# First loads of x in smaller groups, Pool's order of steps, and the place of one weight load in a fused attention and expert kernel

## The chip, the cores and the metric

One core of a Trainium2 chip runs the whole program. Its engines work side by side and meet at semaphores: TensorE (PE, with weight loads as PEld), VectorE (DVE), ScalarE (ACT), GpSimd (Pool) and SyncE (SP), which here only issues DMAs. The metric is the device time of one execution in microseconds (us).

## The reference

The input x is [2, 2048, 256]. Two blocks follow each other, each wrapped as x + layernorm(block(layernorm(x))).

```python
def attn(x):                       # softmax-free attention
    h = layernorm(x) * norm_w + norm_b
    q, k, v = split(h @ qkv_w.T + qkv_b)
    o = (q @ k.T / sqrt(C)) @ v
    return x + o @ proj_w.T + proj_b

def ffn(x):                        # soft mixture of 64 experts, 32 slots each
    logits = einsum('bmd,dnp->bmnp', x, phi)
    dispatch = softmax(logits, axis=0)            # over the batch
    combine = softmax(logits over all n * p)
    slots = einsum('bmd,bmnp->bnpd', x, dispatch)
    y = einsum('bnpd,nde->bnpe', slots, W) + b
    return einsum('bnpd,bmnp->bmd', y, combine)

x = x + layernorm(attn(layernorm(x)))
x = x + layernorm(ffn(layernorm(x)))
```

## The kernel before

Batch b holds 16 tiles of 128 tokens (`NJ` = 16), x lies in `xres[:, b, j, :]`, and t = 16 b + j numbers the 32 tiles. As the attention has no softmax, the kernel builds for each batch the 256 x 256 matrix S of products of normalised rows, and from it and two products of weights (G and U) one matrix A, by which the rows are then multiplied. The stages are:

1. Up to about 46 us: load, statistics, S and the transposed rows, products of weights, A. The change lies here.
2. Up to about 108 us: rows times A (`h_pair`), `add_x`, the norms behind it, the first products with phi.
3. Up to the end: blocks over the experts, then the weighted sum over them and the stores.

Every engine has its own hand-written order of instructions. Nothing is reordered when the program runs; an engine stands at each `wait_ge` until the semaphore is high enough.

**SP** issues loads in this order: five x groups (`X_GROUPS`: tiles 0-1, 2-3, 4-7, 8-11, 12-15 of batch 0; line 352), then `w_raw`, `wbc`, `bbc`, `qbc`, `wpT` (lines 356 to 360, all on `par_loaded`), the four groups of batch 1 (line 352 again), phi (363) and the first expert weights (365). ScalarE's queue issues `proj_b` and `bT` (664, 665).

**VectorE** works through `stats(g)` for each group: one `bn_stats` (L993) and one `bn_aggr` (L996) a tile. Its order is stats 0 to 4, `proj_bias`, `weight_scale` (waits for `par_loaded`; L1008), stats 5, `bias_columns` (six L1002), `primed_weights` (L1036, which gives the first `wprime_ready`), `centre_projection` (L1012 to L1016 on `wpT`, the second `wprime_ready`), stats 6 to 8. After that it takes the largest magnitude of phi, waits for TensorE to spread it (`phi_turn`, `phi_broadcast`), and splits phi into two halves of 16 bits (L1087, L1091). Only then comes the first `add_x` (L1103).

**Pool** turns each group's mean and variance into a scale and an offset in `x_terms(g)`: variance plus epsilon (L504), the power -1/2 (L492), the negative mean (L507), their product (L509, which raises `n1_ready`). Behind all nine groups it runs `residual_terms(b)` for both batches: L516, L517, a power over 16 columns (L492) and the product L521. Their readers are `add_x` and `y_squares` of stage 2. Then come a 16-bit identity and constants for a fold.

**ScalarE** makes the normalised rows: `xhat(t)` (L687) waits for `n1_ready` of its group and, from t = 4, for a free one of four buffers. Its order is xhat(2p), xhat(2p + 1), then the copy of the transposed pair p - 2 (L671). For p = 8 the copy of S of batch 0 stands between these two.

**TensorE** runs 14 warm-up products (`WARM`), then `s_tile(t)` for t = 0 to 31: two products into S (L1453) and two transposes (L1460). Before the transposes of an even tile it waits for the copy of the pair two back. Between the tiles stand the bias rows (after t = 7), `weight_products` and `T_step(0)` (after 17), `R_step(0)` (19), `A_step(0)` (21), `phi_turn` (22) and `phi_broadcast` (24, L1472). `h_pair` (L1511) follows after tile 31.

Of the kernel before, what the change touches and what calls it, by code (L numbers as in the profile page):

```python
# [22 lines left out]
ALU = mybir.AluOpType  # L23
# [4 lines left out]
P = 128  # L28
# [63 lines left out]
def build(nc, x, norm_w, norm_b, qkv_w, qkv_b, proj_wT, proj_b, phi, ffn_w, ffn_bT, out):  # L92
    B, T, C = x.shape
# [3 lines left out]
    NJ = T // P  # L97
# [4 lines left out]
    TB = 512 // P  # L102
    EP = P // Q
    GJ = 4
    XG = B * NJ // GJ
    NG = NJ // GJ
    assert (B, K, TB) == (2, 2, 4)

    x_v = x.rearrange("b (p j) c -> p b j c", j=NJ)
# [7 lines left out]
    with ExitStack() as ctx:  # L117
        def sb(name, shape, dt=F32):
            return ctx.enter_context(nc.sbuf_tensor(name, shape, dt))

        def sem(name):
            return ctx.enter_context(nc.semaphore(name))


        xres = sb("xres", [P, B, NJ, C])
# [44 lines left out]
        wpT = a.take(K * C).rearrange("p (k c) -> p k c", k=K)  # L170
# [53 lines left out]
        mvx = sm.take(64).rearrange("p (b j s) -> p b j s", b=B, j=NJ)  # L224
# [29 lines left out]
        bk = [psM[:, i * 512:(i + 1) * 512] for i in range(4)]  # L254


        par_loaded, rows_loaded = sem("par_loaded"), sem("rows_loaded")
        x_loaded = [sem(f"x_loaded{g}") for g in range(XG + 1)]
        phi_loaded = sem("phi_loaded")
        W_loaded = [sem(f"W_loaded{i}") for i in range(2)]  # L260
        pool_const = sem("pool_const")
# [52 lines left out]
        out_stored = [sem(f"out_stored{i}") for i in range(2)]  # L314

        y_lots = [(1, 0), (1, 1), (0, 0), (0, 1), (1, 2), (0, 2), (1, 3), (0, 3)]
        N_PAR = 5


        X_GROUPS = [(0, 0, 2), (0, 2, 2)] + [(b, j, GJ) for b in range(B) for j in range(0, NJ, GJ) if b + j]  # L320
        GROUP_OF = {(b, j + i): g for g, (b, j, n) in enumerate(X_GROUPS) for i in range(n)}


# [25 lines left out]
        def _(sp):  # L349
            def load_x(g):  # L350
                b, j, n = X_GROUPS[g]
                sp.dma_start(xres[:, b, j:j + n, :], x_v[:, b, j:j + n, :]).then_inc(x_loaded[g], 16)

            for g in range(NG + 1):
                load_x(g)
            sp.dma_start(w_raw, qkv_w.rearrange("(s p) c -> p s c", p=P)).then_inc(par_loaded, 16)
            sp.dma_start(wbc, norm_w.rearrange("(o c) -> o c", o=1).broadcast_to([P, C])).then_inc(par_loaded, 16)
            sp.dma_start(bbc, norm_b.rearrange("(o c) -> o c", o=1).broadcast_to([P, C])).then_inc(par_loaded, 16)
            sp.dma_start(qbc, qkv_b).then_inc(par_loaded, 16)
            sp.dma_start(wpT, proj_wT.rearrange("(k p) e -> p k e", p=P)).then_inc(par_loaded, 16)  # L360
            for g in range(NG + 1, XG + 1):
                load_x(g)
            sp.dma_start(phf, phi_v).then_inc(phi_loaded, 16)
            for w in range(2):
# [93 lines left out]
        def _(pool):  # L458
            own = Count(pool, pool_own)
# [29 lines left out]
            def rsqrt(o, v):  # L489

                n = v.shape[1]
                return nc.gpsimd.tensor_tensor(o, v, epst[:, 0:1].broadcast_to([P, n]), ALU.pow)  # L492
# [3 lines left out]
            def x_terms(g):  # L496

                b, j, n = X_GROUPS[g]
                tn = slice(j, j + n)
                e2, nm = ve[:, g % 2 * 8:g % 2 * 8 + n], ve[:, g % 2 * 8 + GJ:g % 2 * 8 + GJ + n]  # L500
                pool.wait_ge(stats_x, g + 1)
                if g >= 2:
                    pool.wait_ge(n1_ready, g - 1)
                own.add(nc.gpsimd.tensor_scalar(e2, mvx[:, b, tn, 1], 1.0 + EPS, EPS * EPS, ALU.mult, ALU.add))  # L504
                own.wait()
                own.add(rsqrt(r1[:, b, tn], e2))
                own.add(nc.gpsimd.tensor_scalar(nm, mvx[:, b, tn, 0], -1.0, 0.0, ALU.mult, ALU.add))  # L507
                own.wait()
                nc.gpsimd.tensor_tensor(n1[:, b, tn], nm, r1[:, b, tn], ALU.mult).then_inc(n1_ready, 1)  # L509

            def residual_terms(b):

                e1, nm = ve[:, 16:32], ve[:, 32:48]
                if b:
                    pool.wait_ge(r0_ready, b)
                own.add(nc.gpsimd.tensor_scalar(e1, mvx[:, b, :, 1], EPS, 1.0, ALU.add, ALU.mult))  # L516
                own.add(nc.gpsimd.tensor_scalar(nm, mvx[:, b, :, 0], -1.0, 0.0, ALU.mult, ALU.add))  # L517
                own.wait()
                own.add(rsqrt(r0[:, b], e1))
                own.wait()  # L520
                nc.gpsimd.tensor_tensor(n0[:, b], nm, r0[:, b], ALU.mult).then_inc(r0_ready, 1)  # L521

            for g in range(XG + 1):
                x_terms(g)
            residual_terms(0)
            residual_terms(1)
            pool.wait_ge(r0_ready, 2)
            nc.gpsimd.tensor_scalar(ident16, ident, 1.0, 0.0, ALU.mult, ALU.add).then_inc(ident16_ready, 1)
# [132 lines left out]

        @block.scalar
        def _(act):
            act.dma_start(pb_rows[Q - 1:Q], proj_b.rearrange("(o c) -> o c", o=1)).then_inc(rows_loaded, 16)
            act.dma_start(bT[:, :, :], ffn_bT.rearrange("(k p) n -> p k n", p=P)).then_inc(rows_loaded, 16)

# [305 lines left out]
        def _(dve):  # L972
            own = Count(dve, dve_own)
# [12 lines left out]
            def stats(g):  # L986

                b, j, n = X_GROUPS[g]
                dve.wait_ge(x_loaded[g], 16)
                if g >= 2:  # L990
                    dve.wait_ge(stats_x, g - 1)
                for i in range(n):
                    own.add(V.bn_stats(stat[:, g % 2, i, :], xres[:, b, j + i, :]))  # L993
                own.wait()
                for i in range(n):
                    ins = V.bn_aggr(mvx[:, b, j + i, :], stat[:, g % 2, i, :])  # L996
                ins.then_inc(stats_x, 1)
# [7 lines left out]
            def weight_scale():  # L1005

                dve.wait_ge(par_loaded, 16 * N_PAR)
                own.add(V.tensor_tensor(w_aug, w_raw, wbc.unsqueeze(1).broadcast_to([P, KS, C]), ALU.mult))  # L1008

            def centre_projection():  # L1010

                own.add(V.tensor_reduce(wm, wpT, AX_X, ALU.add))  # L1012
                own.wait()
                own.add(V.tensor_scalar(wm, wm, 1.0 / C, None, ALU.mult))
                own.wait()
                V.tensor_tensor(wpT, wpT, wm.unsqueeze(2).broadcast_to([P, K, C]), ALU.subtract).then_inc(wprime_ready, 1)  # L1016

            def proj_bias():

                dve.wait_ge(rows_loaded, 32)  # L1020
                dve.wait_ge(pool_const, 2)
                own.add(V.tensor_reduce(pbm[P - Q:P, 0:1], pb_rows, AX_X, ALU.add))
                own.wait()
                own.add(V.tensor_scalar(pbm[P - Q:P, 1:2], pbm[P - Q:P, 0:1], 1.0 / C, None, ALU.mult))
                own.wait()
                own.add(V.tensor_scalar(pb_rows, pb_rows, pbm[P - Q:P, 1:2], None, ALU.subtract))
# [11 lines left out]
                own.wait()  # L1038
                V.tensor_tensor(w_aug[:, :, C - 1], bcol, qbc, ALU.add).then_inc(wprime_ready, 1)

            stats(0)
            stats(1)
            stats(2)
            stats(3)
            stats(4)
            proj_bias()
            weight_scale()
            stats(5)
            own.add(V.tensor_reduce(bmx, bT.rearrange("p k n -> p (k n)"), AX_X, ALU.max, apply_absolute_value=True))
            bias_columns()  # L1050
            primed_weights()
            centre_projection()
            stats(6)
            stats(7)
            stats(8)

            def pow2_scale(i, top, least, done):

# [768 lines left out]
```

## Time and profile before

| | us |
|---|---|
| median of three runs | 641.18 |
| lowest and highest of them | 640.73, 641.26 |
| the profiled execution, whole | 641.88 |
| its span in the profile | 640.1 |
| TensorE busy in the span | 628.2 |
| VectorE, ScalarE, Pool busy | 447.9, 359.0, 230.2 |

Times in the views count from the start of the span. A line such as L1036 is that line of the kernel. On TensorE, a busy stretch need not be one at full pace, since the ends of its instructions are modelled. The releaser in brackets is inferred from semaphores: it is what came last before an engine went on.

### The profile page before, as it was taken

The numbers are of one execution on the slowest core, as the hardware profiler recorded it, in microseconds if no ns is written. First come the engines' busy times: TensorE is split into PE (matmuls) and PEld (weight loads), VectorE is DVE, ScalarE is ACT, GpSimd is POOL, SyncE is SP. The second block draws the span as 40 slices with busy tenths as digits, with TensorE's granted clock in tenths as the row PEclk, the third lists the DMA queues.
The fourth block names the chain that finished last, engine by engine and source line by source line (L and its number), as shares of the span: only waits on it lengthen the run. The fifth ranks groups of instructions, "written<-read, shape, count | busy, mean of one in ns | idle before, by whom it ended". The sixth has DMA issues, their size and how long they took to land.

```text
span 640.1 us, 15341 instructions
## 1 busy us (share of the span) xinstructions
PE 628.2 (98%) x5351; PEld 395.4 (62%) x5351; DVE 447.9 (70%) x857; ACT 359.0 (56%) x694; POOL 230.2 (36%) x410
## 2 busy tenths in 40 slices
PE   8999999999999999999999999999999999999996
PEld 8898644545444444444444457777777777777776
DVE  5978888835244453446344399999888888888886
ACT  5666776843233232224444356777777777777764
POOL 5375896820000000000000001555555555555554
PEclk9999999999999999999999999999999999999999
DMA  8920032325766666666555531222222222222201
GB/s 266 402 77 1 1 67 50 67 60 156 201 176 176 177 193 185 173 178 203 135 136 186 159 104 67 91 90 90 90 90 90 90 90 90 90 90 90 90 16 34
DMA packets 78485, 77.07 MB, mean 120 GB/s; under 512 B 6386, under 2 KB 74995, under 8 KB 76147
## 3 DMA queue, kind: packets, MB, share of 16 engines
q1 hardware_dynamic: 76112, 74.48, 38.4%
q10 hardware_dynamic: 2338, 2.16, 1.0%
q8 instruction: 19, 0.31, 0.2%
q14 instruction: 16, 0.12, 0.1%
HBM read 51.71 MB, written 23.07 MB: 117 GB/s over the span
## 4 chain that ended last, share of the span: by engine, by line
PE 79%; DVE 8%; POOL 5%; issue 3%; DMA 2%; ACT 2%; SPq 1%; DVEq 0%; POOLq 0%; ACTq 0%
PE psL L1568 24%; PE psM L1555 11%; PE psL L1687 11%; PE psM L1705 7%; PE psM L1709 7%; PE psM L1706 7%; PE psM L1585 3%; POOL small L492 2%; DMA r_xn<-in_proj_wT 2%; PE psL L1773 1%; PE psL L1453 1%; PE psM L1511 1%; DVE phs L1091 1%; DVE small L1286 1%; DVE r_xn L1305 1%
## 5 line engine op out<-in xcount | busy, mean ns | idle before, releaser
L1568 PE MATMUL psL<-r,r_xn 128*128 128x512 f16 x768 | 176.3, 379 | 0.8 <-DVE r L1112 0.8
L1568 PEld LDWEIGHTS psL<-r,r_xn 128*128 128x128 f16 x768 | 73.4, 98 | 91.0 <-issue 7.0
L762 ACT ACTIVATE r<-psM,small 128x512 f32<-128x512 f32 x64 | 43.7, 682 | 96.3 <-PE psM L1555 95.5
L1555 PE MATMUL psM<-phs,xx 128*128 128x512 f16 (+1 forms) x384 | 93.2, 379 | 0.9 <-DVE xx L1146 0.9
L580 POOL MEMSET r_xn<- 128x8 f16 x2 | 0.3, 137 | 234.2 <-PE psL L1568 234.2
L1110 DVE TENSOR_SCALAR r<-r 128x512 f16<-128x512 f32 x64 | 28.5, 445 | 71.8 <-ACT r L762 71.8
L1687 PE MATMUL psL<-phs,r 128*32 128x512 f16 x1344 | 75.1, 379 | 0.0
L1555 PEld LDWEIGHTS psM<-phs,xx 128*128 128x128 f16 x384 | 37.3, 98 | 45.9 <-DVE xx L1146 1.4
L875 ACT ACTIVATE r<-psL,small 128x512 f32<-128x512 f32 x60 | 41.9, 776 | 37.7 <-DVE small L1313 37.4
L492 POOL TENSOR_TENSOR small<-small,epst 128x2 f32<-128x2 f32 (+3 forms) x75 | 59.8, 797 | 6.2
L1687 PEld LDWEIGHTS psL<-phs,r 128*32 128x32 f16 x1344 | 34.6, 97 | 36.5 <-issue 3.0
L875 ACT ACTIVATE r_xn<-r_xn,small 128x512 f32<-128x512 f32 x64 | 47.1, 824 | 1.3 <-DVE small L1313 1.3
L1112 DVE SCALAR_TENSOR_TENSOR r<-r 128x512 f16<-128x512 f32 x64 | 46.1, 721 | 2.2
L597 POOL TENSOR_SCALAR small<-small 128x1 f32<-128x1 f32 x30 | 20.5, 682 | 69.6 <-ACT r L910 69.3
L1286 DVE TENSOR_REDUCE small<-psL 128x1 f32<-128x512 f32 x60 | 38.2, 684 | 6.0 <-PE psL L1687 6.0
L671 ACT ACTIVATE r<-psM 128x512 f32<-128x512 f32 (+1 forms) x67 | 39.1, 585 | 4.8 <-PE psM L1611 3.2
L1272 DVE STREAM_TRANSPOSE xx<-r_xn 128x1024 f32<-128x1024 f32 x32 | 39.1, 1228 | 2.3 <-ACT r_xn L875 1.5
L585 POOL TENSOR_TENSOR r<-xx,r 128x1024 f16<-128x1024 f32 x15 | 32.0, 2136 | 19.8 <-DVE r_xn L1264 19.8
L1305 DVE CUSTOM_DVE_ANT_0 r_xn<-psL,xx 128x512 f32<-128x512 f32 x60 | 37.9, 687 | 1.6 <-issue 0.6
L1272 DVE STREAM_TRANSPOSE r<-r 128x1024 f32<-128x1024 f32 x32 | 38.1, 1225 | 0.5 <-ACT r L875 0.4
L1264 DVE TENSOR_TENSOR r_xn<-r,r_xn 128x1024 f16<-128x1024 f32 x32 | 37.2, 1202 | 0.1
L1232 DVE TENSOR_TENSOR r_y<-psM,r 128x512 f32 (+1 forms) x12 | 8.3, 692 | 41.0 <-PE psM L1585 41.0
(200 smaller groups left out, 1260.8 us busy)
## 6 DMA issues: line engine op xcount, KB each, us to landing
r<-in_ffn_w SPq DMA_DIRECT2D x23, 1024.0 KB, 5.8
logit_difference<-r SPq DMA_DIRECT2D x256, 64.0 KB, 1.9
xx<-logit_difference SPq DMA_DIRECT2D x16, 1024.0 KB, 4.8
out<-r SPq DMA_DIRECT2D x32, 128.0 KB, 1.7
xres<-in_x SPq DMA_DIRECT2D x7, 512.0 KB, 11.4
r<-in_phi SPq DMA_DIRECT2D x1, 2048.0 KB, 19.3
expert_bias<-r ACTq DMA_DIRECT2D x1, 2048.0 KB, 21.6
r<-expert_bias SPq DMA_DIRECT2D x16, 128.0 KB, 5.5
```

The lines of the kernel that those rows point to most:

```text
L492: return nc.gpsimd.tensor_tensor(o, v, epst[:, 0:1].broadcast_to([P, n]), ALU.pow)
L875: nc.scalar.activation(E[b][:, c], src[:, c], ACT.Exp, bias=ebias[:, w, g:g + 1], scale=kap[:, 0:1]).then_inc(E_ready[b], 1)
L1112: V.scalar_tensor_tensor(thl[:, j % 2, 1], tF[:, j % 2], S_SCALE, thl[:, j % 2, 0], ALU.mult, ALU.subtract).then_inc(s_split, 1)
L1272: V.transpose(ET[b].rearrange("p (t g r) -> p g t r", g=GJ, r=Q)[:, g2], E[b].rearrange("p (g t c) -> p g t c", g=GJ, c=Q)[:, g2]).then_in ...
L1286: own.add(V.tensor_reduce(lmax[:, 0, g:g + 1], logits_at(j)[:, 512 * g:512 * g + 512], AX_X, ALU.max))
L1305: V.tensor_tensor_reduce(E0[:, c], logits_at(j)[:, c], dB[:, c], 1.0, -3.0e38, ALU.add, ALU.max, lmax[:, 1, g:g + 1]).then_inc(l_added, 1)
L1555: ins = mm(bk[j % 2][:, :].rearrange("p (q m) -> p q m", q=EP), xxT[:, 1, j, hx, k, :], phw[:, hp, k, :, bass.ds(nb, 1), :].rearrange("p q ...
L1568: ins = mm(psL[:, i * 512:(i + 1) * 512], x3n[:, b, j, hx, k * P:(k + 1) * P], thl[:, j % 2, hs, :], start=(j == 0 and hx + hs == 0), stop ...
L1687: ins = mm(logits_at(j)[q * Q:(q + 1) * Q, g * 512:(g + 1) * 512], xj[:, hx, k, g * Q:(g + 1) * Q], phs[:, hp, k, q * 512:(q + 1) * 512], ...
L1705: mm(acc, eT[b][:, 0, t, :], yh(b, t), start=first, stop=False)
L1706: mm(acc[:, 0:C], eT[b][:, 0, t, :], yl(b, t), start=False, stop=False)
L1709: return mm(acc, eT[b][:, 1, t, :], yh(b, t), start=False, stop=last)
```

## The change

- The groups of x in batch 0 become tiles 0, 1, 2-3, 4-5, 6-7, 8-11, 12-15; those of batch 1 stay. There are eleven groups (`XG`), seven of them in batch 0 (`NG`).
- Tile 1's load is issued from ScalarE's queue, ahead of its two others.
- `wpT` has its own semaphore, `wpT_loaded`. `weight_scale` waits for four loads instead of five, and `centre_projection` waits for `wpT`. On SP the load of `wpT` stands behind batch 1's first group.
- In `x_terms` on Pool the negative mean stands ahead of the power.
- `residual_terms(0)` moves on Pool from behind all groups to behind batch 0's groups.

```diff
+    X_GROUPS = [(0, 0, 1), (0, 1, 1), (0, 2, 2), (0, 4, 2), (0, 6, 2)] + [
+        (b, j, GJ) for b in range(B) for j in range(0, NJ, GJ) if b or j >= 2 * GJ]
+    XG = len(X_GROUPS)
+    NG = XG - NJ // GJ
...
-        N_PAR = 5
-        X_GROUPS = [(0, 0, 2), (0, 2, 2)] + [(b, j, GJ) for b in range(B) for j in range(0, NJ, GJ) if b + j]
+        N_PAR = 4
...
-            for g in range(NG + 1):
-                load_x(g)
+            for g in range(NG):
+                if g != 1:
+                    load_x(g)
...
-            sp.dma_start(wpT, proj_wT.rearrange("(k p) e -> p k e", p=P)).then_inc(par_loaded, 16)
-            for g in range(NG + 1, XG + 1):
+            load_x(NG)
+            sp.dma_start(wpT, proj_wT.rearrange("(k p) e -> p k e", p=P)).then_inc(wpT_loaded, 16)
+            for g in range(NG + 1, XG):
                 load_x(g)
...
                 own.add(nc.gpsimd.tensor_scalar(e2, mvx[:, b, tn, 1], 1.0 + EPS, EPS * EPS, ALU.mult, ALU.add))
+                own.add(nc.gpsimd.tensor_scalar(nm, mvx[:, b, tn, 0], -1.0, 0.0, ALU.mult, ALU.add))
                 own.wait()
                 own.add(rsqrt(r1[:, b, tn], e2))
-                own.add(nc.gpsimd.tensor_scalar(nm, mvx[:, b, tn, 0], -1.0, 0.0, ALU.mult, ALU.add))
                 own.wait()
...
-            for g in range(XG + 1):
+            for g in range(NG):
                 x_terms(g)
             residual_terms(0)
+            for g in range(NG, XG):
+                x_terms(g)
             residual_terms(1)
...
+            act.dma_start(xres[:, 0, 1:2, :], x_v[:, 0, 1:2, :]).then_inc(x_loaded[1], 16)
...
             def centre_projection():
 
+                dve.wait_ge(wpT_loaded, 16)
                 own.add(V.tensor_reduce(wm, wpT, AX_X, ALU.add))
...
-            stats(0)
-            stats(1)
-            stats(2)
-            stats(3)
-            stats(4)
+            for g in range(NG):
+                stats(g)
             proj_bias()
             weight_scale()
-            stats(5)
+            stats(NG)
...
-            stats(6)
-            stats(7)
-            stats(8)
+            for g in range(NG + 1, XG):
+                stats(g)
```

## Rows read from the trace of the kernel before

**Rows 1.** Chain that ended last, in order of time: start us, us, what
```profile
6.06 10.88 DMA r_xn<-in_proj_wT
...
39.39 0.32 PE psM L1472 x2
...
49.55 0.40 DVE r_y L1103
```

**Rows 2.** Timeline, TensorE: start, duration us, line, out<-in, count [idle before <-releaser]
```profile
1.90 5.93 PE L1516 MATMUL psM<-r 128*128 128x128 f32 x28 [1.90 <-POOL r L468]
...
7.67 0.82 PE L1453 MATMUL psL<-r 128*128 128x256 f32 x4
...
8.54 0.82 PE L1453 MATMUL psL<-r 128*128 128x256 f32 x4
...
12.24 0.44 PE L1460 MATMUL psM<-r 128*128 128x128 f32 x2
...
24.84 0.44 PE L1460 MATMUL psM<-r 128*128 128x128 f32 x2 [0.49 <-ACT xx L671]
...
56.68 3.72 PE L1511 MATMUL psL<-r,xx 128*128 128x256 f32 x16 [0.21 <-DVE r L1031]
```

**Rows 3.** Timeline, ScalarE: tiles 16 and 17
```profile
22.78 1.09 ACT L687 ACTIVATE r<-xres,small 128x255 f32<-128x255 f32 x2 [1.22 <-POOL small L509]
```

**Rows 4.** Timeline, VectorE: weight scaling, statistics, bias columns, primed weights
```profile
16.96 1.76 DVE L1008 TENSOR_TENSOR r_xn<-r_xn 128x1536 f32<-128x1536 f32 x1 [3.75 <-DMA r_xn<-in_proj_wT]
...
18.64 1.40 DVE L993 BATCH_NORM_STATS2 stat<-xres 128x6 f32<-128x256 f32 x4
...
20.54 0.41 DVE L1002 CUSTOM_DVE_ANT_0 r<-r_xn 128x256 f32<-128x256 f32 x1
...
22.72 1.75 DVE L1036 TENSOR_TENSOR r_xn<-r_xn 128x1530 f32<-128x1530 f32 x1
```

**Rows 5.** Timeline, Pool: first groups, tile 16's group, residual terms
```profile
5.06 0.19 POOL L504 TENSOR_SCALAR small<-small 128x2 f32<-128x2 f32 x1 [2.85 <-DVE small L996]
...
6.32 0.19 POOL L509 TENSOR_TENSOR small<-small 128x2 f32<-128x2 f32 x1
...
6.60 0.19 POOL L504 TENSOR_SCALAR small<-small 128x2 f32<-128x2 f32 x1
...
8.81 0.20 POOL L504 TENSOR_SCALAR small<-small 128x4 f32<-128x4 f32 x1 [0.78 <-DVE small L996]
...
10.66 0.20 POOL L504 TENSOR_SCALAR small<-small 128x4 f32<-128x4 f32 x1
...
20.54 0.47 POOL L504 TENSOR_SCALAR small<-small 128x4 f32<-128x4 f32 x1 [6.29 <-DVE small L996]
...
22.47 0.27 POOL L509 TENSOR_TENSOR small<-small 128x4 f32<-128x4 f32 x1
...
33.51 0.21 POOL L516 TENSOR_SCALAR small<-small 128x16 f32<-128x16 f32 x1
...
37.38 0.44 POOL L516 TENSOR_SCALAR small<-small 128x16 f32<-128x16 f32 x1
```

**Rows 6.** DMA issues (KB each, median us to landing), then SP's queue in time
```profile
xres<-in_x SPq DMA_DIRECT2D x7, 512.0 KB, 11.4
...
small<-in_qkv_b SPq DMA_DIRECT2D x1, 3.0 KB, 9.1
...
5.52 0.50 SPq L359 DMA_DIRECT2D small<-in_qkv_b  x1
...
6.81 3.51 SPq L352 DMA_DIRECT2D xres<-in_x  x4
```

**Rows 7.** Timeline, Pool and VectorE near 504 us, far behind the change
```profile
504.03 1.28 POOL L601 TENSOR_TENSOR small<-small 128x1 f32<-128x1 f32 x1
...
504.05 1.22 DVE L1264 TENSOR_TENSOR r<-xx,r 128x1024 f16<-128x1024 f32 x1
```

**Rows 8.** Timeline, Pool: terms of x3, mean ahead of power
```profile
54.28 0.19 POOL L552 TENSOR_SCALAR small<-small 128x2 f32<-128x2 f32 x1 [0.60 <-DVE small L1132]
...
55.88 0.19 POOL L539 TENSOR_SCALAR small<-small 128x2 f32<-128x2 f32 x1
```

**Rows 9.** Timeline, VectorE: phi's split, one instruction a row
```profile
40.69 0.48 DVE L1087 TENSOR_SCALAR phs<-r,small 128x512 f16<-128x512 f32 x1
...
41.08 0.48 DVE L1087 TENSOR_SCALAR phs<-r,small 128x512 f16<-128x512 f32 x1
...
44.09 0.75 DVE L1091 SCALAR_TENSOR_TENSOR phs<-r,small,phs 128x512 f16<-128x512 f32 x1
```

More of the change, by code:

```diff
@@ L104, in build @@
     GJ = 4
-    XG = B * NJ // GJ
-    NG = NJ // GJ
+    X_GROUPS = [(0, 0, 1), (0, 1, 1), (0, 2, 2), (0, 4, 2), (0, 6, 2)] + [
+        (b, j, GJ) for b in range(B) for j in range(0, NJ, GJ) if b or j >= 2 * GJ]
+    XG = len(X_GROUPS)
+    NG = XG - NJ // GJ
     assert (B, K, TB) == (2, 2, 4)
@@ L254, in build @@
         bk = [psM[:, i * 512:(i + 1) * 512] for i in range(4)]
-        par_loaded, rows_loaded = sem("par_loaded"), sem("rows_loaded")
-        x_loaded = [sem(f"x_loaded{g}") for g in range(XG + 1)]
+        par_loaded, rows_loaded, wpT_loaded = sem("par_loaded"), sem("rows_loaded"), sem("wpT_loaded")
+        x_loaded = [sem(f"x_loaded{g}") for g in range(XG)]
         phi_loaded = sem("phi_loaded")
```

## The prediction

> **What bounds the kernel now.** I read the chain that ended last in order of time, then the timelines of the engines over its first 50 us. TensorE's work and what it waits for carry the span, and the part that the change touches ends at about 50 us. The chain begins with the landing of `wpT` at 6.06 + 10.88 = 16.94 us, because `par_loaded` counts all five parameter loads. From there it runs through VectorE, Pool and ScalarE to TensorE's tile 16, then along TensorE's own order to the broadcast of phi's top at 39.39, and through VectorE's split of phi to the first `add_x` at 49.55 [rows 1]. On TensorE's timeline the reader sees this [rows 2]. The 14 warm-up products fill TensorE from 1.90 to about 7.6, and tile 0 starts at 7.67. After that one tile takes 8.54 - 7.67 = 0.87 us. There are two visible hold-ups: the transposes of tile 4 start at 12.24, and those of tile 16 at 24.84 after 0.49 us of idle. At tile pace tile 4 would start at 7.67 + 4 x 0.87 = 11.15 and its transposes at 11.8, so about 0.44 us was lost there. At tile 16, `xhat` started at 22.78, waiting for Pool's L509 [rows 3, 5]; that wait ends last.
>
> **The change, part by part.** All sums go against the profiled execution (span 640.1 us, whole run 641.88 us) as a difference, which I then put on the median of 641.18 us.
>
> **Smaller first loads, one of them on ScalarE's queue.** Half a group saves one statistics instruction of 1.40 / 4 = 0.35 us [rows 4] and about 0.1 us of aggregation. Pool's first term then starts at 5.06 - 0.45 = 4.6 us, or 4.2 us if 128 KB also lands 0.4 us sooner. `xhat` of tile 0 is ready some 0.6 us sooner, but tile 0 is queued behind the warm-up to 7.6 us, so nothing is gained at the start. If that cover were gone it would be worth 0.5 to 0.9 us. Against it stands Pool's pace. A group of two costs 6.60 - 5.06 = 1.54 us [rows 5], and there are now five groups ahead of tile 8 where there were three. Tiles 2 and 3 come third on Pool: 4.2 + 3 x 1.6 = 9.0 us against a need at 7.67 + 2 x 0.87 = 9.4 less `xhat`'s 0.59, so TensorE loses about 0.2 us there and wins back part of the 0.44 at tile 4. By tile 8 I count a gain of 0 to 0.5, likeliest 0.1 us, and it dies at tile 16 in any case unless tile 16's terms come sooner too. ScalarE's extra issue of about 0.5 us falls in its idle first 6 us. The two row loads behind it (`proj_b`, `bT`) move by as much; their reader on VectorE stands just ahead of L1008, where VectorE sat idle for 3.75 us [rows 4].
>
> **Pool's negative mean ahead of its power.** The same three steps and the product, in another order. Pool runs one instruction at a time, so nothing is hidden. The later helper already has the new order: 55.88 - 54.28 = 1.60 us a group [rows 8], against 1.54 in the old one [rows 5]. That is +0.06 us a group; the value for `x_terms` is taken as 0 to +0.06.
>
> **Weights' last load behind x of batch 1.** `weight_scale` now waits for four loads. The last of them, `qbc`, was issued at 5.52 and took 9.1 us: 14.6 us [rows 6]. SP issues one x load more ahead of it but the bytes in front are the same, so 14.6 to 15.1. VectorE's L1008 moves from 16.96 to about 14.65 and ends at 14.65 + 1.76 = 16.4 [rows 4]. Next comes `stats` of the first group of batch 1. Of the seven 512 KB loads the median landing, 11.4 us, is the fourth issued, which went out at 6.81: 18.2 us [rows 6], 1.27 us behind `wpT` for 512 KB. With `wpT`'s 256 KB behind it rather than ahead it lands about 0.63 us sooner: 17.6 (to 18.2). So stats start at 17.6 rather than 18.64 and are ready for Pool at 17.6 + 1.9 = 19.5 rather than 20.54 [rows 4, 5]. `wpT` then lands at 18.2, and its reader is due after 23 us: free. VectorE's L1036 keeps its distance of 22.72 - 18.64 = 4.08 us from these stats and so runs from 21.7 to 23.4 [rows 4].
>
> **`residual_terms(0)` ahead of batch 1's terms.** It costs Pool 37.38 - 33.51 = 3.87 us [rows 5]; it leaves a place where nobody waited for it and enters a place ahead of tile 16's terms. A group of four takes 10.66 - 8.81 = 1.85 us today [rows 5], 1.91 in the new order, so Pool ends batch 0's terms near 4.2 + 2 x 1.56 + 3 x 1.6 + 2 x 1.9 = 15.9 us (1.56 for a group of one is an estimate between the two orders). If nothing disturbed it the residual terms would end at 19.8, just as tile 16's statistics are ready. But now L1008 runs beside Pool. Far behind, near 504 us, the trace shows what that does: a Pool product of one column, of 0.19 us on quiet ground (L509 at 6.32) [rows 5], took 1.28 us beside a VectorE product with two SBUF inputs of 1.22 us, and both ended together [rows 7]. L1008 is of that kind, and used to run within the 6.29 us in which Pool stood idle [rows 5]. Pool's L509 of the last group, due at about 15.7, therefore ends at about 16.55. The residual terms run from 16.65 to 20.5, and tile 16's terms start at 20.5, no sooner than today.
>
> From there today's distance to L509 is 22.47 - 20.54 = 1.93 us [rows 5], which gives 22.45. Today L509 slips in 0.25 us ahead of L1036. After the change L1036 starts at 21.7 and L509 falls into it: it ends at about 23.55. `xhat` of tile 16 starts at 23.6 rather than 22.78, **0.82 us later**, and TensorE's transposes with it. TensorE is dense from there to phi's broadcast, so the delay stays.
>
> The Trainium skill, "SBUF — State Buffer", section "Who interferes with whom", says that a VectorE instruction with two SBUF inputs and a GpSimd instruction that reads SBUF exclude each other for the whole instruction. By that rule the trace agrees, with 1.28 us; without such a lock the change would come out at the first rival below.
>
> **What comes back.** Pool's last terms, identity and fold constants end up to 3.87 + 1 us sooner, with the residual terms gone from their front, and so leave phi's split alone. L1087's pace is 41.08 - 40.69 = 0.39 us where Pool is quiet, but the eight took 44.09 - 40.69 = 3.40 us [rows 9]: 0.28 us is returned. TensorE's h pairs see +0.82 less the 0.21 us for which TensorE waits for VectorE at 56.68 today [rows 2], so 0.54 to 0.61 whichever of the two is late there. **The sum** for what follows is +0.82 - 0.25 = about +0.6 us. Later stages hang on these engines and not on loads, so I carry it unchanged: 641.18 + 0.6 = 641.8 us.
>
> **Rivals.** First, Pool is not held up: L1008 lands on Pool's long power, which takes its inputs at once. Then tile 16's terms start at 19.5 to 19.8, `xhat` at 21.75 to 22.0, and by today's distance of 24.84 - 22.78 = 2.06 us [rows 2, 3] TensorE's transposes at 23.8 to 24.1, 0.75 to 1.0 us sooner. What is late next is S's copy behind tile 15, so 0.5 to 0.95 us; with 0.25 from phi's split, 640.0 to 640.4. For it speaks that VectorE's six L1002 (22.72 - 20.54 = 2.18 us [rows 4]) ran undelayed beside a Pool power; against it that the short steps come between. Second, and on the other side: the power of tile 16's terms itself comes behind L1036. It is issued 0.85 us after the terms start, at 21.35, with L1036 at 21.7. If Pool is over 0.35 us later than I count, or x lands that much sooner, the power waits to 23.4 and L509 ends at 24.85: +2.1 - 0.25 = 1.85 us, so 643.0. Third, batch 1's x lands at 18.4 or later, L1036 starts behind L509, and only the 0.25 of phi's split is left: 640.9. Last, the loads don't land sooner at all, `qbc`'s small packets being the limit: L1008 near 15.5, everything 0.8 us later on Pool, L509 behind L1036 at 24.0 or so: +1.0, 642.2.
>
> **How the numbers follow.** Chances: forecast 0.42 (641.4 to 642.4), first rival 0.20, slower rival 0.20, third 0.10, last 0.08. The range 640.0 to 643.1 takes in the ends of all but some 0.2. A difference under 0.2% (1.28 us) is about what a measurement of this kernel can't tell from no change. Beyond it on the fast side lies about half of the first rival, with a little for load times that I can't see: 0.13. Beyond it on the slow side lie the slower rival and the upper tails of the forecast and of the last: 0.27. The rest, 0.60, is no difference.
>
> **What would show it.** In the profile of the changed kernel: tile 0 at 7.67 as today; L1008 near 14.7; a Pool L509 of over 0.8 us beside it; the residual terms ending at about 20.5; another long L509 beside L1036, ending near 23.5; `xhat` of tile 16 at 23.6; phi's eight L1087 in 3.2 us; the first `add_x` some 0.5 us later than 49.47. The forecast is wrong if Pool's steps beside L1008 and L1036 keep their 0.2 us, or if tile 16's terms start before 20 us.

## The result: slower by 0.4%

| | median us | lowest to highest | runs | ratio to before, 95% interval |
|---|---|---|---|---|
| before | 641.18 | 640.64 to 641.63 | 7 | |
| changed | 643.97 | 642.38 to 645.08 | 7 | 1.0044 [1.0032, 1.0055] |

The changed kernel takes 2.8 us more, where 0.6 was forecast and 643.1 was the upper end. Its runs also spread over 2.7 us where those of before spread over 1.0. The profiled execution took 643.97 us, with a span of 642.0. One execution of a later kernel, at a mean clock of 0.852, took 728.45 us and is in no median here.

Pool's timeline (start us, duration us, line, instruction) holds the cause. L512 is the last step of a group's terms, L519 to L524 are the residual terms of batch 0, and L507 is the first step of tile 16's terms:

```profile
14.85 1.01 POOL L495 TENSOR_TENSOR small<-small,epst 128x4 f32<-128x4 f32 x1
15.94 1.79 POOL L512 TENSOR_TENSOR small<-small 128x4 f32<-128x4 f32 x1
17.81 0.20 POOL L519 TENSOR_SCALAR small<-small 128x16 f32<-128x16 f32 x1
...
21.36 0.35 POOL L524 TENSOR_TENSOR small<-small 128x16 f32<-128x16 f32 x1
21.80 1.68 POOL L507 TENSOR_SCALAR small<-small 128x4 f32<-128x4 f32 x1
23.56 0.20 POOL L508 TENSOR_SCALAR small<-small 128x4 f32<-128x4 f32 x1
23.84 1.01 POOL L495 TENSOR_TENSOR small<-small,epst 128x4 f32<-128x4 f32 x1
24.92 0.29 POOL L512 TENSOR_TENSOR small<-small 128x4 f32<-128x4 f32 x1
```

VectorE's timeline of the same stretch has the two long products of the weights, `weight_scale` and `primed_weights`:

```profile
15.91 1.76 DVE L1014 TENSOR_TENSOR r_xn<-r_xn 128x1536 f32<-128x1536 f32 x1 [2.14 <-DMA small<-in_qkv_b]
17.58 1.40 DVE L999 BATCH_NORM_STATS2 stat<-xres 128x6 f32<-128x256 f32 x4
...
21.67 1.75 DVE L1043 TENSOR_TENSOR r_xn<-r_xn 128x1530 f32<-128x1530 f32 x1
```

Two Pool steps that take 0.2 us elsewhere took 1.79 and 1.68 us: each lasted until the VectorE product beside it had ended (at 17.67 and 23.42). Together they are 3.1 us longer than quiet ones. Beside the statistics, which read one tile from SBUF and not two, L519 took its usual 0.20 us. The terms of tile 16 were ready at 25.2 instead of 22.74 [rows 5]. ScalarE and TensorE follow:

```profile
25.24 1.09 ACT L693 ACTIVATE r<-xres,small 128x255 f32<-128x255 f32 x2 [3.59 <-POOL small L512]
```

```profile
25.90 1.65 PE L1456 MATMUL psL<-r 128*128 128x256 f32 x4 [2.31 <-ACT r L693]
27.34 0.65 PE L1463 MATMUL psM<-r 128*128 128x128 f32 x2
27.79 1.45 PE L1456 MATMUL psL<-r 128*128 128x256 f32 x4
29.07 0.39 PE L1463 MATMUL psM<-r 128*128 128x128 f32 x2
29.29 1.89 PE L1440 MATMUL psM<-r_xn 128*128 128x256 f32 x8
```

`xhat` of tile 16 is 25.24 - 22.78 = 2.46 us later than before [rows 3]. TensorE then runs two tiles at half pace: the four records of a tile's first products last 1.65 and 1.45 us where they took 0.82 [rows 2]. The stages show why (stretch, length, then busy time and count of TensorE, its weight loads, VectorE, ScalarE and Pool, then the granted clock, the DMA share and GB/s):

```profile
23.50:25.90 2.40, 0.09 (x2) 0.01 (x1) 2.33 (x7) 0.66 (x2) 1.49 (x3) 0.95 1.05 390
25.90:26.90 1.00, 1.00 (x2) 0.84 (x3) 0.97 (x7) 1.00 (x4) 0.00 (x0) 0.50 1.06 381
26.90:27.90 1.00, 1.00 (x6) 0.94 (x5) 1.00 (x4) 1.00 (x3) 0.77 (x3) 0.50 1.09 392
27.90:28.90 1.00, 1.00 (x5) 0.82 (x5) 0.96 (x7) 0.81 (x2) 0.84 (x3) 0.50 1.09 389
```

After 2.31 us without work the granted clock was 0.50, the lower of the two levels (1.2 of 2.4 GHz), for some 3 us. From the transposes of tile 16 to the products of weights TensorE needed 29.29 - 27.34 = 1.95 us. Before, these products began at 25.98 on the same view, 1.14 us behind the transposes [rows 2]:

```profile
25.98 1.89 PE L1437 MATMUL psM<-r_xn 128*128 128x256 f32 x8
```

So the clock costs 0.81 us, and TensorE is 2.5 + 0.8 = 3.3 us late. That lateness is still there at the start of stage 2:

```profile
52.59 1.65 DVE L1106 SCALAR_TENSOR_TENSOR r_y<-xres,small,psM 128x256 f32<-128x256 f32 x4
```

The first `add_x` starts 52.59 - 49.47 = 3.12 us later. The missing 0.2 us is phi's split, undisturbed by Pool.

At the end the spans of the two profiled executions differ by only 1.9 us, though the medians differ by 2.8. The profiled execution of before (641.88 us, 0.7 over its median) carries a wait of TensorE of 0.92 us in stage 2, and a second one of 0.27 us at 95.44, that the changed kernel's lacks: 3.1 - 1.2 = 1.9. The first row is before, the second the run with primed_weights alone in pieces, below, which has it too:

```profile
91.11 1.47 PE L1555 MATMUL psM<-phs,xx 128*128 128x512 f16 x6 [0.92 <-DVE xx L1146]
```

```profile
90.95 1.47 PE L1559 MATMUL psM<-phs,xx 128*128 128x512 f16 x6 [0.92 <-DVE xx L1150]
```

The other profiled executions don't have the wait at 91 us. The run with the residual terms back, for one, has TensorE at the same point as before at 78 us (77.92 against 77.97), and its span is 638.9 us against 640.1. So one profiled execution of a kernel can stand 1 us from another, and the medians are the measure here. What decides whether this wait comes was not tested.

### The profile page after: what moved, and what is told of

Same layout as the page of the kernel before. It is cut to its first block, busy times and chain, and to the rows that moved or that the text cites. A ratio compares the mean times of both kernels' runs of the same rounds, so it can differ in the third digit from the quotient of the medians.

```text
span 642.0 us, 15355 instructions
## 1 busy us (share of the span) xinstructions
PE 628.8 (98%) x5351; PEld 395.9 (62%) x5351; DVE 447.7 (70%) x857; ACT 359.0 (56%) x694; POOL 231.7 (36%) x418
## 4 chain that ended last, share of the span: by engine, by line
PE 81%; POOL 7%; DVE 6%; issue 3%; ACT 1%; DMA 0%; POOLq 0%; DVEq 0%; ACTq 0%
PE psL L1571 24%; PE psM L1558 11%; PE psL L1690 11%; PE psM L1708 7%; PE psM L1712 7%; PE psM L1709 7%; PE psM L1588 3%; POOL small L495 3%; PE psL L1456 2%; PE psM L1514 1%; PE psL L1776 1%; PE psL L1514 1%; DVE small L1289 1%; POOL r_xn L568 1%; DVE r_xn L1308 1%
## 5 line engine op out<-in xcount | busy, mean ns | idle before, releaser
L602 POOL TENSOR_SCALAR small<-small 128x1 f32<-128x1 f32 x30 | 20.6, 686 | 69.6 <-ACT r L916 69.3
```

## Experiments

**Theory A:** a Pool instruction that reads SBUF waits out a VectorE instruction with two SBUF inputs. The change brings Pool into two such products one after the other: the sooner `weight_scale` meets the end of batch 0's terms, the residual terms hand the delay on to tile 16's terms, and these fall into `primed_weights`. The rivals were the order of the loads, the small groups with Pool's pace, the residual terms as such, and (for the last 0.8 us) something other than the clock. Medians of before beside these runs were 641.01, 640.96 and 641.04.

### The residual terms back in their place

```diff
-            for g in range(NG):
+            for g in range(XG):
                 x_terms(g)
             residual_terms(0)
-            for g in range(NG, XG):
-                x_terms(g)
             residual_terms(1)
```

> The changed kernel with residual_terms(0) put back on Pool behind all groups; the rest of the change stays. In the changed kernel the first step of tile 16's terms (L507) started at 21.80 and took 1.68 us beside VectorE's L1043, and xhat of tile 16 started at 25.24 against 22.78 before. Theory A (Pool is held up by VectorE products with two inputs from SBUF, and the residual terms push tile 16's terms into the second of them): tile 16's terms start at 19.5 and are through before 21.7, xhat of tile 16 starts at 21.6 to 21.8, TensorE keeps its clock, and the time is 0.5 to 1.2 us below before: 640.0 to 640.7. Rival B (the smaller first groups or the new order of loads cost the time): L507 of tile 16 still ends after 23 us and the time stays near 643 to 644.

640.83 us, ratio 0.9998 [0.9989, 1.0007]: all of the loss is gone, but the time is above the expected 640.0 to 640.7. Pool still meets the first product and is then free in time for tile 16's statistics:

```profile
16.02 1.28 POOL L512 TENSOR_TENSOR small<-small 128x4 f32<-128x4 f32 x1
19.06 0.47 POOL L507 TENSOR_SCALAR small<-small 128x4 f32<-128x4 f32 x1 [1.76 <-DVE small L1000]
```

ScalarE started `xhat` of tile 16 at 21.63, as Theory A said. But the gain of 0.5 to 1.2 us that I expected from it didn't come. TensorE's transposes of tile 16 started at 24.80, against 24.84 before, because ScalarE's next copies wait for tile 15:

```profile
23.70 0.55 ACT L675 ACTIVATE r_xn<-psL 128x128 f32<-128x128 f32 x2 [0.99 <-PE psM L1461]
24.14 0.60 ACT L675 ACTIVATE xx<-psM 128x512 f32<-128x512 f32 x1
```

The two copies of S can't start before tile 15 is done, and the copy of transposed pair 6, on which TensorE's transposes wait, stands behind them. In the trace of before, tile 15 was done at 23.10 + 0.38 = 23.48 and the copies of S started at 23.77, so at most 0.3 us was to be had:

```profile
23.10 0.38 PE L1460 MATMUL psM<-r 128*128 128x128 f32 x2
```

```profile
23.77 0.52 ACT L671 ACTIVATE r_xn<-psL 128x128 f32<-128x128 f32 x2
```

Sooner terms for tile 16 are worth next to nothing. Later ones cost in full: in the profiled executions with `xhat` of tile 16 at 22.78 or later and these copies in their old order, the transposes start 2.06 us behind it (2.10 in the changed kernel, where the clock fell).

### The residual terms alone, on the kernel before

```diff
-            for g in range(XG + 1):
+            for g in range(NG + 1):
                 x_terms(g)
             residual_terms(0)
+            for g in range(NG + 1, XG + 1):
+                x_terms(g)
             residual_terms(1)
```

> The kernel before with residual_terms(0) alone moved on Pool to behind batch 0's groups. Theory A: Pool was idle from 14.25 to 20.54, so the residual terms run from 14.3 to about 18.2; only their last product meets L1008 (16.96 to 18.7) and ends by 18.8, ahead of tile 16's statistics at 20.5. xhat of tile 16 stays at 22.8; with Pool quiet during phi's split 0.1 to 0.3 us is gained: 640.9 to 641.1. Rival C (the move of the residual terms costs by itself, wherever VectorE's products stand): xhat of tile 16 later than 23.5 and 642.5 or more.

640.82 us, ratio 0.9996 [0.9987, 1.0005], against 641.01. The gain of 0.19 us is of the size expected and inside the noise (the time is 0.1 us under the expected range). Pool's one meeting with L1010 (16.67 to 18.4) cost 0.58 - 0.22 = 0.4 us where nobody waited:

```profile
17.93 0.58 POOL L521 TENSOR_TENSOR small<-small 128x16 f32<-128x16 f32 x1
20.25 0.47 POOL L504 TENSOR_SCALAR small<-small 128x4 f32<-128x4 f32 x1 [1.74 <-DVE small L998]
```

So the move is harmless by itself; it did harm only together with the sooner `weight_scale`.

### wpT's place alone, on the kernel before

```diff
-            sp.dma_start(wpT, ...).then_inc(par_loaded, 16)
-            for g in range(NG + 1, XG + 1):
+            load_x(NG + 1)
+            sp.dma_start(wpT, ...).then_inc(wpT_loaded, 16)
+            for g in range(NG + 2, XG + 1):
                 load_x(g)
```

Not shown: `weight_scale` waits for four loads, `centre_projection` for `wpT_loaded`, as in the changed kernel.

> The kernel before with wpT's load alone moved behind batch 1's first group and taken out of par_loaded (one semaphore of its own). Theory A: the products weight_scale start at 15 to 16 us, batch 1's first statistics at 17.6, Pool's terms of tile 16 at 19.5, xhat of tile 16 at 21.5 to 21.8. What is late next is the copy of S behind tile 15 (ends 23.3), so TensorE gains 0.4 to 0.6 us and the time is 640.4 to 640.8. Rival B: the new order of loads costs the time: xhat of tile 16 not sooner than 22.8 and the time 641.2 or more.

640.91 us, ratio 1.0001 [0.9991, 1.0010]. `weight_scale` started at 15.09 and `xhat` of tile 16 at 21.86, about as Theory A said (21.5 to 21.8), but TensorE again waited 0.48 us for the same copy (transposes at 25.02). The expected 0.4 to 0.6 us didn't come (the time is above 640.4 to 640.8), for the reason found in the first run. The order of loads doesn't cost anything either.

### VectorE's two long products in six pieces each

```diff
-                own.add(V.tensor_tensor(w_aug, w_raw, wbc..., ALU.mult))
+                for s in range(KS):
+                    own.add(V.tensor_tensor(w_aug[:, s, :], w_raw[:, s, :], wbc, ALU.mult))
...
-                own.add(V.tensor_tensor(w_aug[:, :, 0:C - 1], ..., ALU.subtract))
+                for s in range(KS):
+                    own.add(V.tensor_tensor(w_aug[:, s, 0:C - 1], w_aug[:, s, 0:C - 1],
+                                            w_aug[:, s, C - 1:C]..., ALU.subtract))
```

> The changed kernel with VectorE's two long products (weight_scale L1014 and primed_weights L1043, 1.75 us each) written as six products of 256 columns each. The work is the same. Theory A (whoever holds the shared ports holds them for one instruction): Pool's steps beside them take at most 0.5 us instead of 1.79 and 1.68, the terms of tile 16 end near 22.5, xhat of tile 16 starts at 22.3 to 22.9, TensorE keeps its clock, and the time is within 0.5 us of before: 640.7 to 641.5. Rival D (Pool waits for VectorE's whole stretch, or for something else that comes with it): the steps stay at 1.5 us or more, xhat of tile 16 at 25 us, 643 to 644.

640.73 us, ratio 0.9999 [0.9990, 1.0009]: every part of the change is in place, and its whole loss is gone. VectorE is 2.12 us over the first product instead of 1.76 (15.43 to 17.55), and 2.09 over the second (from 21.61). Pool's steps:

```profile
15.98 0.28 POOL L512 TENSOR_TENSOR small<-small 128x4 f32<-128x4 f32 x1
16.34 0.26 POOL L519 TENSOR_SCALAR small<-small 128x16 f32<-128x16 f32 x1
...
20.34 0.25 POOL L507 TENSOR_SCALAR small<-small 128x4 f32<-128x4 f32 x1
20.67 0.27 POOL L508 TENSOR_SCALAR small<-small 128x4 f32<-128x4 f32 x1
21.02 1.07 POOL L495 TENSOR_TENSOR small<-small,epst 128x4 f32<-128x4 f32 x1
22.17 0.26 POOL L512 TENSOR_TENSOR small<-small 128x4 f32<-128x4 f32 x1
```

The first two and the last two of these rows stand beside pieces, for the power of tile 16's terms (21.02) in part. The same work in shorter instructions leaves them 0.05 to 0.08 us of delay a step; in the later runs with pieces a short step beside them took up to 0.46 us. The two rows between (0.25 and 0.27 us) stand beside the bias columns, VectorE instructions of 0.4 us that also read two inputs from SBUF. It is the length of the single VectorE instruction that Pool waits out. The Trainium skill says so in "SBUF — State Buffer", section "Who interferes with whom" (the pair is held for the whole instruction), and the run agrees for VectorE as the holder. For Pool's power as the holder the runs differ from it, and they decide (last section).

### Only one of the two products in pieces

> The changed kernel with only primed_weights' product (the later one) in six pieces. Theory A: the first collision stays (a Pool step of 1.3 to 1.8 us beside weight_scale), so tile 16's terms start near 21.3 to 21.8 as in the changed kernel, but no step beside primed_weights takes over 0.5 us: xhat of tile 16 at 23.3 to 23.9, 1.4 us sooner than 25.24, TensorE idle under 1 us and its clock kept: 641.3 to 642.2. Rival K: one collision is as dear as both: 643 or more.

> The changed kernel with only weight_scale's product (the sooner one) in six pieces. Theory A: Pool is through batch 0's terms and the residual terms by about 20.0 to 20.4, tile 16's terms start at 20.4 and their last step (L512) is due at 22.2, beside primed_weights (21.6 to 23.4), so it takes about 1.2 us: xhat of tile 16 at 23.5 (the course that the prediction forecast). 641.3 to 642.2. Rival L: the first product is the whole cause, and without that delay nothing meets the second: xhat of tile 16 at 22.5, 640.7 to 641.0.

Only `primed_weights` in pieces: 641.59 us, ratio 1.0015 [1.0006, 1.0025]. Only `weight_scale` in pieces: 641.51 us, ratio 1.0011 [1.0002, 1.0019]. Both are in the ranges expected. By the medians each of these kernels loses about 0.5 us, where the one with both products whole loses 2.8. With only `weight_scale` in pieces the second meeting stands alone:

```profile
20.17 0.34 POOL L524 TENSOR_TENSOR small<-small 128x16 f32<-128x16 f32 x1
20.60 1.68 POOL L507 TENSOR_SCALAR small<-small 128x4 f32<-128x4 f32 x1
```

Tile 16's terms started at 20.6, near the 20.4 expected, but it was their first step that fell behind the product, not their last: the loads had landed sooner, `weight_scale` ran from 14.37, and `primed_weights` started at 20.47 instead of 21.6. So the second meeting comes in full without the first. `xhat` came at 24.05 instead of 23.5, 3.58 us behind the start of `primed_weights`, as in the changed kernel (25.24 - 21.67 = 3.57): once the first step is held, only the place of this product counts.

In the other run the first meeting was shorter than expected (L512 0.84 us, with `weight_scale` from 14.75), and `xhat` came at 22.79, sooner than the 23.3 expected. The transposes of tile 16 started at 24.85, so in this profile the first meeting cost TensorE nothing; its time of 641.88 us has the wait at 91 us. One execution of each of the two kernels (643.88 and 643.91 us) had a mean clock of 0.997, as the slower ones of the changed kernel, so a fall of the clock seems not to need both meetings. How the 2.8 us of the medians split between the two meetings, the landing of the loads and the clock isn't shown.

### TensorE kept busy while it waits

```diff
             for t in range(B * NJ):
+                if t == NJ:
+                    for i in range(9):
+                        mm(bk[0][:, 0:P], ident[:, :], ident[:, :], start=True, stop=True)
                 s_tile(t)
```

> The changed kernel with nine more warm-up products (128 columns each, 0.21 us at full pace, about 1.9 us in all) on TensorE between tiles 15 and 16, where it stood idle for 2.31 us. They compute nothing that is used. Theory A2: the two tiles behind the idle time ran at the lower clock (granted 0.50 from 25.9 to 28.9, a tile's first products 1.65 us instead of 0.82), and that cost comes on top of the 2.46 us by which xhat of tile 16 was late. With TensorE busy the clock stays at 1.0, tile 16's transposes wait for ScalarE to about 27.3 and the products of weights start at 28.4 instead of 29.3: 0.8 to 0.9 us less than the changed kernel, about 643.1 by its median of 643.97. Rival E: the clock is not what costs there, or falls all the same: no difference from the changed kernel, 643.7 to 644.2.

642.68 us, ratio 1.0029 [1.0020, 1.0039], 1.3 us less than the changed kernel (1.1 with each against its own before), with useless work added. The clock stayed at 1.00 from 23.5 to 30 (one stretch of it, columns as above), and the way from the transposes to the products of weights is 27.94 - 26.79 = 1.15 us again:

```profile
25.90:26.90 1.00, 0.51 (x4) 0.30 (x3) 0.96 (x7) 1.00 (x4) 0.37 (x2) 1.00 1.08 390
```

```profile
26.79 0.44 PE L1463 MATMUL psM<-r 128*128 128x128 f32 x2 [0.49 <-ACT xx L677]
27.06 0.82 PE L1456 MATMUL psL<-r 128*128 128x256 f32 x4
27.72 0.38 PE L1463 MATMUL psM<-r 128*128 128x128 f32 x2
27.94 1.89 PE L1440 MATMUL psM<-r_xn 128*128 128x256 f32 x8
```

So 0.8 us is the clock. Between the two profiled executions (643.97 and 642.64 us) the other 0.5 is a sooner landing in this one (L1014 at 15.39, `xhat` at 24.73). Its runs span 642.17 to 643.36; the two fastest of the seven of the changed kernel, at 642.38 and 643.09, had a mean clock of 0.998 and 0.999, and the other five, with 0.996 and 0.997, took 643.75 to 645.08. So much of the changed kernel's spread seems to be whether the clock falls; another part is where the loads land.

### The first groups as before, the rest changed

```diff
-    X_GROUPS = [(0, 0, 1), (0, 1, 1), (0, 2, 2), (0, 4, 2), (0, 6, 2)] + [
-        (b, j, GJ) for b in range(B) for j in range(0, NJ, GJ) if b or j >= 2 * GJ]
+    X_GROUPS = [(0, 0, 2), (0, 2, 2)] + [(b, j, GJ) for b in range(B) for j in range(0, NJ, GJ) if b + j]
```

Not shown: tile 1's load goes back to SP with the rest of its group.

> The changed kernel with the first loads of x in groups of two, two and four tiles as before, all from SP; wpT's place, the order on Pool and the place of the residual terms stay changed. Theory A (two collisions in a row, for which Pool has to be late): Pool ends batch 0's terms at 14.4 instead of 15.9 and passes the first steps of the residual terms before weight_scale starts near 15.3, so only one step meets each long product or none, tile 16's terms start at 18.7 to 19.5 and end before L1043 starts at 21: xhat of tile 16 before 22 us and 640.6 to 641.2. Rival F (the residual terms ahead of batch 1's cost whatever stands before them, once the statistics come sooner): xhat of tile 16 at 23.5 or later, 642 or more.

> The same kernel as the run with the groups undone, for its profile alone. Theory A: where the parameter loads land decides. In this profile the two last steps of batch 0's and the first of the residual terms pass before weight_scale starts, tile 16's terms start at 18.5 to 19.5, no Pool step beside a long product takes over 0.6 us, and the time is 640.5 to 641.2; if the loads land as soon as 14.3 to 14.9 one step of 1.3 us or more stands beside weight_scale, tile 16's terms start over 1 us later, and the time is 641.5 to 642.5.

641.07 us, ratio 1.0003 [0.9994, 1.0012], but in two courses: eight of its runs took 640.34 to 641.57 and three 642.05 to 642.42. Its first profile (of the execution at 728.45 us, where only the course of Pool and VectorE up to tile 16 is read) has no short step beside a long product. Pool was in its power when `weight_scale` started at 15.55, tile 16's terms started at 19.13, and `xhat` at 21.66:

```profile
15.18 2.90 POOL L493 TENSOR_TENSOR small<-small,epst 128x16 f32<-128x16 f32 x1
```

The second profile (641.77 us) is of the slower kind, as expected for a sooner landing: Pool got as far as the second residual step before `weight_scale` (14.95) started, and later the power of tile 16's terms fell behind `primed_weights` (20.76):

```profile
15.21 1.59 POOL L518 TENSOR_SCALAR small<-small 128x16 f32<-128x16 f32 x1
16.89 2.90 POOL L493 TENSOR_TENSOR small<-small,epst 128x16 f32<-128x16 f32 x1
...
20.85 2.52 POOL L493 TENSOR_TENSOR small<-small,epst 128x4 f32<-128x4 f32 x1
```

2.52 us against 1.01 to 1.07 is what the prediction's slower rival described. `xhat` came at 23.69. The groups are thus a part of the cause: with the longer queue of small groups a step of Pool met `weight_scale` in every profile taken; with the old ones it depends on where the loads land.

### The order of Pool's steps as before, the rest changed

```diff
-                own.add(nc.gpsimd.tensor_scalar(nm, mvx[:, b, tn, 0], -1.0, 0.0, ALU.mult, ALU.add))
                 own.wait()
                 own.add(rsqrt(r1[:, b, tn], e2))
+                own.add(nc.gpsimd.tensor_scalar(nm, mvx[:, b, tn, 0], -1.0, 0.0, ALU.mult, ALU.add))
```

> The changed kernel with the negative mean behind the power again in x_terms. Theory A: the 0.06 us a group that the new order costs (1.60 against 1.54 in rows) make Pool about 0.4 us sooner by the seventh group, but it then waits for the end of weight_scale (17.7) just the same, so tile 16's terms start at 21.7 as before and fall behind L1043 again: 643.4 to 644.4, no difference from the changed kernel beyond the noise. Rival G: the lateness of 0.35 us by the new order is what lets the collision happen: xhat of tile 16 before 23 us and 641 to 642.

642.15 us (640.27 to 645.15), ratio 1.0016 [1.0004, 1.0027]. I expected no difference from 643.97, and the median is 1.8 us lower: a miss. The mechanism is the same and the profile has both meetings (L510 1.60 us at 14.92, L507 1.57 us at 20.76). VectorE's side of it:

```profile
14.71 1.76 DVE L1014 TENSOR_TENSOR r_xn<-r_xn 128x1536 f32<-128x1536 f32 x1 [1.20 <-DMA small<-in_qkv_b]
16.38 1.40 DVE L999 BATCH_NORM_STATS2 stat<-xres 128x6 f32<-128x256 f32 x4
...
20.47 1.81 DVE L1043 TENSOR_TENSOR r_xn<-r_xn 128x1530 f32<-128x1530 f32 x1
```

`xhat` came at 24.38, and TensorE's idle time was 1.79 us with no fall of the clock. Measured from the start of `weight_scale`, `xhat` is no sooner than in the changed kernel (9.67 us against 9.33): with the negative mean behind the power a third step, L510, took 0.66 us at 23.40, beside VectorE's L1023. So in this profile the gain is the landing, 1.2 us sooner, and the clock. How much of the 1.8 us between the medians is the order of the steps stays open: two of the twelve runs, at 640.27 and 640.35, show no loss at all, and neither was profiled.

### S's copy behind the pair's copy

```diff
-                if p == 8:
-                    S_copy(0)
                 if p >= 2:
                     xT_copy(p - 2)
+                if p == 8:
+                    S_copy(0)
```

> The changed kernel with the two long products of VectorE in six pieces each (as in the run with split products) and ScalarE's copy of S of batch 0 put behind the copy of the transposed pair 6 instead of ahead of it. In every run so far with xhat of tile 16 in time TensorE still waited 0.48 us for that pair's copy (24.61 in the run with split products), behind the two copies of S (0.43 us). Theory H: that order is what holds tile 16 once Pool is in time; swapped, the wait falls to 0.1 us or less and all that follows comes 0.3 to 0.45 us sooner: 640.3 to 640.5 against 640.73. Rival I: the wait returns at the next step (the first transposition of S, or a later stage): no difference from 640.73.

> The kernel before with two moves only: residual_terms(0) behind batch 0's groups on Pool, and ScalarE's copy of S of batch 0 behind the copy of the transposed pair 6. Loads, groups, order of Pool's steps and VectorE's products are as before. Theory H: the whole gain of the best run so far (640.26) is from the copy of S and from Pool's quiet during phi's split, and the loads, groups and split products give nothing: 640.2 to 640.5 (the residual terms alone gave 640.82), TensorE's wait at tile 16 below 0.2 us. Rival J: the sooner statistics by wpT's place are needed for it: 640.7 or more.

On top of the changed kernel with split products: 640.26 us, ratio 0.9989 [0.9980, 0.9998]. On the kernel before, with the residual terms moved and nothing else: **640.12 us, ratio 0.9987 [0.9979, 0.9996]**, the lowest median, though the two can't be told apart. Both gains are small, with intervals that end just short of no difference. In the second kernel's profile TensorE no longer waits at tile 16, and its transposes start 0.69 us sooner than before (in the first at 24.32, 0.52 us sooner):

```profile
23.28 0.82 PE L1455 MATMUL psL<-r 128*128 128x256 f32 x4
24.15 0.44 PE L1462 MATMUL psM<-r 128*128 128x128 f32 x2
```

The loads, the groups and the order of Pool's steps add nothing to it. The last wait at tile 16 was ScalarE's own order, which the change didn't touch.

## Why the prediction was wrong, step by step

- **Right: the mechanism.** A long Pool L512 beside L1014, the residual terms ending late, and a second long step beside L1043 were forecast, with the stretch of the VectorE instruction as their price. The run with the products in pieces shows that this is the cause.
- **The step that failed: "L509 falls into it", for +0.82 us.** I had the last of tile 16's four steps meet L1043. The first step met it, and all four came behind: L507 1.68 us, `xhat` at 25.24 instead of 23.6, +2.46 us. Two terms of the sum were wrong, and they make up the 1.64 us between.
- **First term: where the parameters land (1.26 us).** L1014 was put at 14.65, its loads at 14.6 to 15.1. It started at 15.91, its last load `qbc` still the one waited for. In the other profiled executions with `wpT` moved it began at 14.32 to 15.55. In this course `xhat` goes with it: it starts 9.33 us behind L1014 here and 24.73 - 15.39 = 9.34 in the run with TensorE kept busy.
- **Second term: the wait for x of batch 1 (the other 0.38 us).** The prediction let the statistics wait for x until 17.6, and so put L1043 21.7 - 14.65 = 7.05 us behind L1014. In every profile with `wpT` moved they follow L1014 without such a wait (16.38 behind a product from 14.71, in the rows of the run with the old order of steps), and L1043 starts 5.76 to 5.81 us behind L1014 where that is whole (21.67 - 15.91 = 5.76 here). Pool, once held to L1014's end, needs 21.71 - 15.91 = 5.8 us to the end of the residual terms. So tile 16's first step comes beside L1043 wherever the loads land, and after a first meeting that lasts to L1014's end its last step can't be the only one to meet L1043.
- **Luck: 17.6.** The statistics at 17.58 and L1043 at 21.67 match the forecast of 17.6 and 21.7, but only because L1014's lateness took the place of a wait for x that wasn't there. Only the distance between the two (4.09 against 4.08) was right for its reason.
- **The slower rival** described the course that came, with a price of +2.1 us for `xhat`. It had the chance of 0.20, too little for a margin of 0.35 us when the landing was known no better than to 0.5.
- **Not thought of: TensorE's clock.** The prediction carried the delay through a TensorE that kept its pace. In the idle time of 2.31 us, where before it had 0.49, the clock fell, for 0.81 us more. Without it the result would be about 643.2, at the range's end of 643.1.
- **Wrong in its size: the first rival's gain.** It and two later expectations credited sooner terms for tile 16 with 0.4 to 1.2 us. "S's copy behind tile 15" was named as what is late next, but the rows of before leave it only 0.3 us (23.48 against 23.77), and the early gains that would have brought tile 15 forward didn't come. With `xhat` of tile 16 0.9 to 1.15 us sooner TensorE gained nothing (transposes at 24.80 and 25.02 against 24.84).
- **The early part:** tiles 1 and 2 each waited for Pool (0.31 and 0.46 us), and the bias rows began at 15.33 against 15.22 before. The gain there is -0.1 us where 0 to 0.5 was given. Tile 0 began at 6.72, not 7.67, because the warm-up products took 4.94 us and not 5.93 in that execution (4.75 to 6.22 in the other profiles); with the gaps behind it, it was worth nothing, as said.
- **What comes back:** phi's eight L1090 took 3.25 us against 3.36 as displayed, and from the pow2 steps to the first `add_x` 0.19 us was returned, where 0.28 was forecast.

## What to carry to other kernels

Before an engine's work is moved to "idle" time, look up what runs on VectorE in the new place: if that is one long instruction with two SBUF inputs, a Pool step of 0.2 us costs up to the whole of it, and a chain that is made late once can fall into the next. Writing such a product in pieces costs a fifth more on VectorE and takes most of the hazard away (0.46 us was the longest short step left). And ask what is late next before a sooner result is priced: here the copy order on ScalarE made 1 us of sooner `xhat` worth nothing, while swapping two copies gave 0.5 and 0.7 us by the medians (640.73 to 640.26 and 640.82 to 640.12) and 0.3 and 0.5 us at TensorE's transposes (24.61 to 24.32 and 24.67 to 24.15).

## What the runs showed of the hardware that I had not expected

- The granted clock fell to 0.50 in 2.31 us of idle of a TensorE that had worked for 21 us with no pause over 0.46 us, and stayed there for 3 us of full work. In the run with 1.79 us of idle and, after one short burst, another 0.49, it stayed at full level in the profiled execution.
- Pool's power that is already running is not a hindrance for VectorE: with only `primed_weights` in pieces, `weight_scale` started at 14.75, beside a power that ran from 14.64 to 15.65, and took its usual 1.76 us. So it did with the residual terms alone moved, from 16.67 beside a power of 16 columns from 14.96 to 17.86. A power that has yet to start waits like any other step (2.52 instead of 1.07 us).
- Where a 3 KB load lands behind some 3 MB of others differs from one profiled execution to another by up to 1.6 us (`weight_scale` at 14.32 to 15.91, over eleven profiles with `wpT` moved). In the two of the kernel with the old groups, 15.55 and 14.95 went with two courses whose times stand some 1.4 us apart.
